# Graph layers on one core: gathers released by the count of activations, column lists in larger loads

## The reference

```python
h = (x_flat @ W_gat).reshape(M, HEADS, NUM_EXPERTS)
e = leaky_relu(a_src[src] + a_dst[dst])
ee = exp(e - segment_max(e, dst)[dst])
alpha = ee / (segment_sum(ee, dst)[dst] + 1e-16)
agg = segment_sum(h[src] * alpha, dst)            # per node, over its in-edges
scores = layernorm(agg).mean(over heads)          # 4 experts
topk_s, topk_i = top_k(scores, 2); w = softmax(topk_s)
for ei in range(4):
    g = where(topk_i == ei, w, 0).sum(-1)
    out += g * (gelu(x @ W1[ei] + b1[ei]) @ W2[ei] + b2[ei])
```

## Time and profile before

| | us |
|---|---|
| runs, median of 3 | 2968.47 (2968.46 to 2982.97) |
| profiled execution | 2942.29 |
| its span, first to last instruction | 2940.4 |
| TensorE busy with matmuls | 2209.8 (75%) |
| VectorE busy | 1547.2 (53%) |
| GpSimd busy | 1506.0 (51%) |
| ScalarE busy | 814.3 (28%) |
| `experts_and_attention` begins | about 1637 |

### The profile page before, as it was taken

The page is one execution under the profiler, slowest core; times in us unless marked ns, Lnnn a source line. Parts: engine busy times, 40 slices in busy tenths (PEclk is TensorE's granted clock), DMA queues, the critical chain, the costliest instruction groups (busy, mean ns, idle before and its releaser), DMA issues. The chain is left out here.

```text
span 2940.4 us, 31189 instructions
## 1 busy us (share of the span) xinstructions
PE 2209.8 (75%) x10560; PEld 1468.6 (50%) x10560; DVE 1547.2 (53%) x3199; ACT 814.3 (28%) x1333; POOL 1506.0 (51%) x1497
## 2 busy tenths in 40 slices
PE   2588886888898888888887447885799876686563
PEld 2355664555555555555566325563566544454342
DVE  7566655545655565555478324543564344454235
ACT  2233443223333333333244101100112232232221
POOL 0555664565555666565345566665630545455610
PEclk9799998999999999999998668886899988897786
DMA  7854547343333444333333312211211222254342
GB/s 222 263 173 149 148 131 273 112 117 114 112 113 117 120 127 124 111 110 101 96 122 96 93 28 36 36 37 24 39 37 39 62 69 65 54 176 119 109 132 89
DMA packets 254294, 315.64 MB, mean 107 GB/s; under 512 B 83564, under 2 KB 208298, under 8 KB 251054
## 3 DMA queue, kind: packets, MB, share of 16 engines
q0 software_dynamic: 61008, 123.13, 16.5%
q1 hardware_dynamic: 138424, 117.89, 13.3%
q10 hardware_dynamic: 54694, 72.52, 7.3%
HBM read 237.88 MB, written 75.52 MB: 107 GB/s over the span
## 5 line engine op out<-in xcount | busy, mean ns | idle before, releaser
L785 POOL DMA_INDIRECT c_xg<-xb_dram,src x784 | 789.0, 1006 | 528.5 <-PE ps_a L825 226.4
L2307 POOL DMA_INDIRECT er<-row_dram,gi x608 | 577.9, 950 | 279.7 <-issue 185.2
L2419 PE MATMUL ps_em<-zT_all,ewts 128*128 128x512 f32 (+1 forms) x832 | 403.2, 635 | 128.3 <-ACT hid L2477 78.2
L2429 PE MATMUL ps_en<-ewts,hid 128*128 128x256 f32 x1568 | 350.6, 381 | 6.4 <-issue 6.4
L2429 PEld LDWEIGHTS ps_en<-ewts,hid 128*128 128x128 f32 x1568 | 300.0, 192 | 68.5 <-issue 30.0
L2419 PEld LDWEIGHTS ps_em<-zT_all,ewts 128*128 128x128 f32 x832 | 168.9, 215 | 330.9 <-issue 216.9
L2477 ACT ACTIVATE hid<-ps_em,eb 128x512 f32<-128x512 f32 (+1 forms) x208 | 135.3, 662 | 661.0 <-PE ps_em L2419 366.4
L812 PE MATMUL ps_e<-c_we,c_eaT 64*128 64x256 f32 x1568 | 239.3, 423 | 78.3 <-DVE c_xg L1141 49.8
L2714 DVE TENSOR_TENSOR eo<-ps_en,eb_r 128x1024 f32<-128x1024 f32 (+1 forms) x52 | 60.4, 1162 | 436.8 <-remote 324.4
L1141 DVE TENSOR_TENSOR c_xg<-ps_e,c_xg 128x1024 f32<-128x1024 f32 x196 | 235.6, 1216 | 16.7 <-issue 4.9
L994 ACT ACTIVATE c_xg<-c_xg 128x1024 f32<-128x1024 f32 x196 | 203.9, 1052 | 114.9 <-issue 58.3
(11 more groups left out here) (316 smaller groups left out, 2876.3 us busy)
## 6 DMA issues: line engine op xcount, KB each, us to landing
c_eaT<-in_eaT SPq DMA_DIRECT2D x196, 128.0 KB
eo_dram<-eo ACTq DMA_DIRECT2D x48, 512.0 KB
ewts<-eo_dram ACTq DMA_DIRECT2D x24, 1024.0 KB
c_xg<-xb_dram,src POOLq DMA_INDIRECT x784
c_xl<-xn_dram SPq DMA_DIRECT2D x24, 512.0 KB
c_xm<-xm_dram SPq DMA_DIRECT2D x24, 512.0 KB
erow<-c_none ACTq DMA_DIRECT2D x1, 10240.0 KB
er<-row_dram,gi POOLq DMA_INDIRECT x608
```

The source lines that it names most:

```text
L785: pool.indirect_dma_start(xg[:, k % NB, b, :], None, M["xb_dram"], bass.IndirectOffsetOnAxis(ap=M["src1"][:, k * B + b:k * B + b + 1], axi ...
L2307: pool.indirect_dma_start(er[:, r, b, :], None, M["row_dram"], bass.IndirectOffsetOnAxis(ap=gi[:, r, b:b + 1], axis=0)).then_inc(s_get[r], 16)
L2419: y = pe.matmul(ps_m[n % NM][:, 0:w], w1(x)[:, k, c * P:(c + 1) * P], xT[:, k, at], start=(k == 0), stop=(k == KD - 1))
L2429: y = pe.matmul(ps_n[b][:, t, :], hid[:, b, c, t * P:(t + 1) * P], w2(x)[:, c, :], start=(c == 0), stop=(c == KE - 1))
```

## The change

Two things are changed in the 36 written-out rounds. The pace is no longer `s_pace` with each addition of VectorE. GpSimd waits before every second block (k even, k over `LEAD` = 6) until `s_ge`, ScalarE's count of finished activations, has reached 6(k-6)//5, so gathers are let go in groups of two blocks, eight indirect DMAs. The first eight blocks are free. The rounds in the loop have no such wait any more. And the column lists of four rounds (16 blocks, 32 KB) come in one load into one half of a new `gi`; the lists of the looped rounds keep small loads into `gl`, the first four of them issued at the start.

```diff
+    HELD = 4
+    LEAD = 6
-        gi = sb("gi2", [P, R, MB], I32)
+        gi = sb("gi2", [P, 2, HELD * R, MB], I32)
+        gl = sb("gl2", [P, R, MB], I32)
+        s_lists = [sem(f"s_lists{b}") for b in range(2)]
-        s_pace = sem("s_pace4")
-        AHEAD = 4
 ...
                 for j in range(FIXED):
-                    pool.wait_ge(s_pace, j + 1)
-                    pool.sem_inc(s_go, 1)
                     for r in range(R):
-                        pool.wait_ge(s_idx[r], 16 * j + 16)
-                        pool.sem_inc(s_go, 1)
+                        k = j * R + r
+                        if k % 2 == 0 and k > LEAD:
+                            pool.wait_ge(s_ge, 6 * (k - LEAD) // 5)
+                        if j % HELD == 0 and r == 0:
+                            pool.wait_ge(s_lists[j // HELD % 2], 16 * (j // HELD // 2 + 1))
                         if j:
                             pool.wait_ge(s_put[r], 16 * j)
-                            pool.sem_inc(s_go, 1)
-                        rows_of(r)
+                        pool.sem_inc(s_go, 1)
+                        rows_of(r, gi[:, j // HELD % 2, j % HELD * R + r, :])
                         if j * R + r in BEHIND:
                             slots_of(BEHIND[j * R + r])
 ...
                 with pool.Fori(FIXED, last) as j:
-
-                    pool.wait_ge(s_pace, j + 1)
-                    pool.sem_inc(s_go, 1)
 ...
             def _(sp):
+                def lists_of(q):
+                    sp.dma_start(gi[:, q % 2, :, :], M["order"][q * HELD * ROUND:(q + 1) * HELD * ROUND, :].rearrange("(k p b) o -> p k (b o)", p=P, b=MB)).then_inc(s_lists[q % 2], 16)
 ...
+                for q in range(2):
+                    lists_of(q)
                 for r in range(R):
-                    list_of(0, r)
+                    sp.sem_inc(s_idx[r], 16 * FIXED)
+                    list_of(FIXED, r)
 ...
                 for j in range(FIXED):
                     for r in range(R):
                         store(j, r)
-                        list_of(j + 1, r)
+                    if (j + 1) % HELD == 0 and j + 1 + HELD < FIXED:
+                        lists_of((j + 1) // HELD + 1)
 ...
                     nc.vector.tensor_tensor(eo[:, b, 0:T, :], ps_n[b][:, 0:T, :], b2[:, x, None, :].broadcast_to([P, T, D]), ALU.add).then_inc(s_e, 1)
-                    dve.sem_inc(s_pace, 1)
 ...
-                dve.sem_inc(s_pace, AHEAD)
-                dve.sem_inc(s_pace, E2 // (R * P * MB))
```

More of the change, by code:

```diff
@@ L2121, in experts_and_attention @@
     BLOCK = P * MB
+    HELD = 4
+    assert FIXED % HELD == 0
     AT_DEG = (KC + 1) // 2
+    LEAD = 6
     AT_OFF = AT_DEG + 1
@@ L2303, in _, with rows_of @@
                                         base=0, pattern=[[1, P]], channel_multiplier=-1).then_inc(s_const, 1)
-                def rows_of(r):
+                def rows_of(r, at):
                     for b in range(MB):
                         pool.indirect_dma_start(er[:, r, b, :], None, M["row_dram"],
-                                                bass.IndirectOffsetOnAxis(ap=gi[:, r, b:b + 1], axis=0)).then_inc(s_get[r], 16)
+                                                bass.IndirectOffsetOnAxis(ap=at[:, b:b + 1], axis=0)).then_inc(s_get[r], 16)
                 def gather(j, r):
@@ L2315, in gather @@
                     pool.sem_inc(s_go, 1)
-                    rows_of(r)
+                    rows_of(r, gl[:, r, :])
                 def slots_of(h):
@@ L2363, in _ @@
             def _(sp):
+                def lists_of(q):
+                    sp.dma_start(gi[:, q % 2, :, :], M["order"][q * HELD * ROUND:(q + 1) * HELD * ROUND, :].rearrange("(k p b) o -> p k (b o)", p=P, b=MB)).then_inc(s_lists[q % 2], 16)
                 def list_of(j, r):
-                    sp.dma_start(gi[:, r, :], M["order"][bass.ds((j * R + r) * (P * MB), P * MB), :].rearrange("(p b) o -> p (b o)", p=P)).then_inc(s_idx[r], 16)
+                    sp.dma_start(gl[:, r, :], M["order"][bass.ds((j * R + r) * (P * MB), P * MB), :].rearrange("(p b) o -> p (b o)", p=P)).then_inc(s_idx[r], 16)
                 def store(j, r):
```

## The result

On the chip the changed kernel took 2997.57 us (median of 13 executions, 2971.08 to 3026.23) against 2979.87 us for the kernel before on the same chip (13 executions, 2945.67 to 2998.35). The ratio is 1.0078, 95% interval 1.0049 to 1.0108: slower by 0.8%. The mean times differ by 23.2 us and the medians by 17.7; without the executions that lie over 1.5% above the fastest of their kernel (two of the changed one, one of before) the means still differ by 20.6. The profiled execution took 2977.49 us, with a span of 2975.6 us; that of before had 2940.4. So the two profiles lie 35.2 us apart.

What follows compares the result with a forecast made beforehand. Unbroken rows of gathers starving TensorE were taken as the bound. +48 for activations 9 to 93, -8 at the start, +4 at the end, 0 for tail and lists gave +44 on 2968.5: 3012 us, range 2912 to 3045.

Steps and rivals of the forecast that it cites:

- Seven turns of 77.0 us: Activations 9 to 93: seven times three steps with gather rows of 16, 8, 16; 534 us against 486.3, +48.
- the lone eight: Row of eight gathers released at a step's third activation, standing alone; 16.1 us until the next release.
- The recovery of 3.0 us: After a row's last gather ends, TensorE was taken to need 3.0 us until full speed returns.
- Seventy pairs: Beside a row of gathers, TensorE was taken to do 70 weight-load and matmul pairs at speed before standing still.
- the first rival: If about 84 pairs or more pass, a row of sixteen costs at most 8.0 us; 2913 us, chance 0.18.
- Start: Before activation 9: 56 free gathers in place of 64, 10 us earlier, less 2 for later lists; -8.
- The bound beside it: Upper limit for the first gather's delay by the larger list loads: 8 x 1.77, given as some 13 us.
- End: After activation 93: blocks 84 to 86 run beside step 22, 12 gathers, 17.7 us against 13.4; +4.
- The tail: From 2272.1 us on: the new wait never binds there, so the 668.3 us are carried over; nothing.
- Lists: 144 loads of 2 KB become 9 of 32 KB; removing them was put at 0.
- The rule of the Trainium skill: By it the gathers' place would not matter and the change would be worth 0; step times spoke against it.
- The difference to the median: The median of runs lay 26.2 us above the profiled execution; left as is, giving 2968.5+44 = 3012.

Runs made afterwards that it cites:

- e11: The changed kernel with every second counting matmul left out; one profile, 2933.91 us.
- e1: The kernel before with only the new column-list loads, keeping its old pace; ratio 1.0004 to the kernel before.
- e3: The changed kernel releasing sixteen gathers at a time, once the second activation of each step is done; ratio 1.0248 to the kernel before.
- e2: The changed kernel with GpSimd also waiting, before each pair of blocks, until the gathers of the block before have landed; ratio 0.9452 to the kernel before.
- e4: The changed kernel without the 288 gathers of blocks 14 to 85, all waits, list loads and stores kept; ratio 0.935 to the kernel before.
- e14: The kernel of e2 with the `eo` stores of steps 2 to 21 issued by SyncE in place of ScalarE; ratio 0.9463 to the kernel before.

## Why the prediction came out as it did

The sign was right, the mechanism was right, and the size was too large: +44 us forecast, +35.2 in the profiles, +23.2 by the means. Of the profiles' difference -5.3 us is chance, the earlier end of the stages ahead; the stage itself and the tail cost 40.5.

- *Seven turns of 77.0 us.* The rows are 16, 16, 8 as worked out, and a full turn took 75.1 to 78.6 us, 76.4 in the mean of six; the one with the short step took 69.6, 7 less. Sum 528 against 534. The pieces, in the mean of the six full turns: 30.3 us from c1 (29.6 forecast), 30.9 from c2 (31.3), 15.3 for the lone eight (16.1), so each was near and the errors partly cancelled. The recovery of 3.0 us held in nine of the fourteen rows of sixteen; in four it was 0.2 to 2.4, and once TensorE waited for ScalarE instead. The up matmuls behind a standstill took 8.2 to 9.9 us, where one value, 8.68, had been taken. Not foreseen were the two waits for ScalarE's `hid`, 9.9 us.
- *Seventy pairs.* 65 to 76 pairs passed before the fall, so the first rival (84 or more) did not come. e11 shows that the fall moves with the pairs.
- *Start.* -14.0 in place of -8. The last of the 56 free gathers ended at 1708.8 in place of 1722.2. The first began at 1636.90, 2.9 us earlier instead of 2 later: it waited 4.19 us for its list (1.77 before), so that term had the right size (2.4 for 2), but GpSimd came to it 5.3 us sooner, which is no merit of the change. (The bound beside it, 8 x 1.77, is 14.2 and not 13; nothing rests on it but the far end of the range.)
- *End.* Blocks 84 to 86 beside step 22: +7.8 in place of +4. The row of twelve ran from 2250.35 to 2265.0, and its standstill was followed by slower matmuls (granted clock 0.94 in that stretch, 1.00 before; 53.2 us of matmuls in place of 49.7), which I had left out.
- *The tail.* -0.4 us. The new wait never bound there.
- *Lists: 0.* e1: 1.0004.
- *The rule of the Trainium skill*, page "SBUF — State Buffer", section "SBUF: two separate sides", by which a DMA and compute cannot slow each other: as a rule of SBUF's ports no run here tests it, but the change was not worth 0, as it would have been by that rule. With and without the 288 gathers the 84 activations take 528 and 324 us, and in eights with a pause 403.
- *The difference to the median.* This step was mis-sized. I took the 26 us between the profiled execution and the median as common to both kernels. Against the means of the 13 executions the profiled one of before was 32.7 us short and that of the changed kernel 20.7, so the difference is 12 us less than the profiles say. The double rows may be the reason: the trace of before has one, e1 with the same pace has three, the changed kernel, whose release counts activations, has none in its trace. Three traces don't show it, and single executions of each kernel scatter by some 15 us (standard deviation) in any case.

Block 86 came in step 22, at 2265, the wait before the slots fell from 104.2 to 42.6 us, and the standstills of whole rows were 9 to 12.5 us: near what was put down.

## What to carry to other kernels

A helper engine with time to spare can still be the bound through what it does to the others; its busy share does not show that, the "issue" waits of the engine beside it do. Ask then not how many of its operations there are or how fast they go, but how long they run without a break: here eight gathers and a pause of 2.3 us made both kernels 5 to 6% faster, where another release without a pause cost 0.8% (the change) and 2.5% (e3). And before a difference is forecast from one profile, look for accidents in it (a step twice as long as its neighbours) and ask whether other executions have more of them.

## What the runs showed of the hardware that I had not expected

- A pause of 2.3 us is enough for TensorE (1 us of starved counting), although behind a row of sixteen it came back only 3.0 us after the last gather; a pause of 1.7 us leaves 21 us of it.
- The starvation is not TensorE's alone. ScalarE's first activation of a step came late beside rows of eight although its matmuls were done, and TensorE stood up to 7.4 us for it in e2. With the counting at full speed this is what is left: 403 us up to activation 93 where 324 are possible (e4). Why is open, as said at e14.
- GpSimd itself has holes of 2.0 us inside a row now and then (ahead of 1784.14 in e1). In e1 both rows of the stretch with a hole ran together with the next, in the kernel before neither did.
